# Attention and a routed feed-forward layer on one core: the ScalarE and VectorE programs of attention written out for all 64 heads, and the last stage's weights, tokens and first masks prepared inside attention

## The reference

```python
xn = layernorm(x)
q, k, v = (xn @ W.T + b for each)            # 16 heads of 16 features, q scaled by 1/4
att = softmax(q @ k.T) @ v @ Wo.T + bo       # per batch and head, over 2048 keys
route = top2-masked softmax(xn @ wg + bg), divided by its sum over the batches
seq_ids = top_k(route per expert and batch, 1024)
out = scatter-add over 16 experts of gelu(xn @ w1 + b1) @ w2 + b2     # 64 hidden units each
x + att + layernorm(xn + out) * gamma + beta
```

## Time and profile before

| | |
|---|---|
| three runs | 3382.39, 3384.15, 3384.7 us (median 3384.15) |
| the profiled execution | 3384.77 us |
| its span, first to last instruction | 3383.0 us |
| busy in the span | TensorE 97%, VectorE 86%, ScalarE 75%, GpSimd 28% |
| mean granted TensorE clock | 0.989 of full speed |
| attention, first to last score matmul | 257.5 to 2913.4 us |
| first matmul of the last stage | 2925.1 us |
| loads of weight pieces, issue to landing (median) | 256 KB 7.9 us, 512 KB 9.0 us |
| VectorE's reciprocal of the last sums, 128x512 | 3.35 us |

### The profile page before, as it was taken

The page is one execution under the profiler, slowest core; times in us unless marked ns, Lnnn a source line. Parts: engine busy times, 40 slices in busy tenths (PEclk is TensorE's granted clock), DMA queues, the critical chain, the costliest instruction groups (busy, mean ns, idle before and its releaser), DMA issues. The chain is left out here.

```text
span 3383.0 us, 75004 instructions
## 1 busy us (share of the span) xinstructions
PE 3289.2 (97%) x20848; PEld 1702.7 (50%) x20848; DVE 2901.3 (86%) x2989; ACT 2524.3 (75%) x5724; POOL 933.5 (28%) x1340
## 2 busy tenths in 40 slices
PE   7999999999999999999999999999999999799998
PEld 6444444444444444444444444444444444488887
DVE  7758899999999999999999999999999998377777
ACT  3557788888888888888888888888888888544333
POOL 2550222222222222222222222222222222244443
PEclk9999999999999999999999999999999999899999
DMA  5783333333333333333333333333333332455554
GB/s 197 200 236 47 54 55 54 55 54 55 55 59 58 57 57 59 59 55 59 55 55 54 54 54 55 54 54 55 54 55 57 58 58 42 117 158 158 166 158 118
DMA packets 140694, 271.93 MB, mean 80 GB/s; under 512 B 30192, under 2 KB 76336, under 8 KB 128112
## 3 DMA queue, kind: packets, MB, share of 16 engines
q1 hardware_dynamic: 138144, 266.71, 37.4%
q10 hardware_dynamic: 2256, 1.36, 0.2%
HBM read 173.59 MB, written 84.93 MB: 76 GB/s over the span
## 5 line engine op out<-in xcount | busy, mean ns | idle before, releaser
L921 DVE TENSOR_REDUCE half_max<-m_ps 128x1 f32<-128x1024 f32 x2006 | 2363.5, 1220 | 223.9 <-PE m_ps L848 212.0
L802 ACT ACTIVATE prob<-s_ps 128x512 f32<-128x512 f32 (+1 forms) x5120 | 2191.1, 521 | 425.6 <-PE s_ps L858 417.0
L858 PE MATMUL s_ps<-q_feat,k_feat 50*128 50x512 f32 (+1 forms) x5120 | 1542.9, 397 | 13.8 <-ACTq L792 5.9
L848 PE MATMUL m_ps<-k_feat,q_feat 48*128 48x512 f32 x4012 | 1358.8, 444 | 20.3 <-DVE half_max L921 20.2
L858 PEld LDWEIGHTS s_ps<-q_feat,k_feat 50*128 50x128 f32 x5120 | 798.8, 185 | 994.7 <-ACT prob L802 880.9
L867 PE MATMUL a_ps<-prob,v_head 128*32 128x512 f32 x8192 | 1096.2, 607 | 0.0
L848 PEld LDWEIGHTS m_ps<-k_feat,q_feat 48*128 48x128 f32 x4012 | 599.0, 186 | 221.7 <-DVE half_max L921 211.3
L657 POOL TENSOR_TENSOR shift<-row_max,shift 128x16 fp32r<-128x16 f32 x63 | 14.0, 222 | 1164.1 <-ACT shift L809 1164.1
L867 PEld LDWEIGHTS a_ps<-prob,v_head 128*32 128x32 f32 x8192 | 161.4, 108 | 256.3 <-issue 217.8
L1221 ACT ACTIVATE g_hi<-g 128x512 fp32r<-128x512 f32 x128 | 81.0, 632 | 251.0 <-DVE g L1263 210.8
L1385 POOL TENSOR_TENSOR g_lo<-g,g_hi 128x512 fp32r<-128x512 f32 x128 | 173.5, 1355 | 224.3 <-ACT g_hi L1221 224.2
(11 more groups left out here) (147 smaller groups left out, 2000.5 us busy)
## 6 DMA issues: line engine op xcount, KB each, us to landing
q_feat<-q_parts SPq DMA_DIRECT2D x384, 128.0 KB, 4.2
k_feat<-k_parts SPq DMA_DIRECT2D x384, 128.0 KB, 5.6
q_parts<-parts SPq DMA_DIRECT2D x32, 512.0 KB, 4.3
k_parts<-parts SPq DMA_DIRECT2D x32, 512.0 KB, 4.4
att_dram<-att SPq DMA_DIRECT2D x64, 256.0 KB, 6.3
mask_bc<-mask_b SPq DMA_DIRECT2D x128, 128.0 KB, 4.5
x_in<-in_x SPq DMA_DIRECT2D x16, 512.0 KB, 4.2
xn_dram<-xn SPq DMA_DIRECT2D x16, 512.0 KB, 4.8
```

Source lines behind the costliest of these rows:

```text
L802: act.activation(prob[tile(r, kt) % R][:, cols(j)], s_ps[slot(r, kt, j) % R][:, wide(j)], ACT.Exp).then_inc(exped, 1)
L848: ins = pe.matmul(m_ps[p % 2][:, k * BLK:(k + 1) * BLK], q_feat[r % 2][LOW, qt * P:(qt + 1) * P], k_feat[r % 2][LOW, key:key + BLK], start ...
L858: pe.matmul(s_ps[slot(r, kt, j) % R][:, wide(j)], k_feat[r % 2][UP, kt * P:(kt + 1) * P], q_feat[r % 2][UP, cols(j)], start=True, stop=Tru ...
L921: dve.tensor_reduce(half_max[r][:, p // 2, p % 2:p % 2 + 1], m_ps[p % 2][:, :], AX.X, ALU.max).then_inc(maxed, 1)
```

## The change

ScalarE's program of attention becomes one line of 64 written-out heads, and VectorE's writes out the maxima of heads 2 to 63; both loops go. The loops of TensorE, GpSimd and SyncE stay.

The tensors of the last stage that can be filled early are laid over `v_all`: its memory is taken, released, and taken again by `w1_hi`, `w2_lo`, `w2_hi`, `xn_hi0`, `xn_lo0`, `woT_sb`, `wo_hi`, `gamma_bc`, `w1_lo`, `mask_bc0` and `b1_col`. SyncE loads w1 (1 MB) and b1 in attention after its loop, ahead of head 61's loads, and w2 (1 MB) after the mask is there, then block 0's tokens and mask quarter 0. VectorE rounds and splits both weights at the end of its attention program. In `finish` the six pieces and TensorE's waits for them are gone. SyncE's order at its start is new: it waits for the store of the last head's sums, loads the sums, then issues mask quarter 1, `quotients(0)`, `halves(1, 1)`, `tokens(0)`, and waits for b2's parts. VectorE inverts the sums in four quarters (two after gate 1, two after gate 2) and splits them after gates 3, 4 and 5.

```diff
+SUMS_AT = 4 * S
+INV_AT = SUMS_AT + BLK
+LATE_AT = INV_AT + PARTS * BLK // 2
...
+        with nc.sbuf_tensor("v_all", [P, B, H, ST, HD], F32) as v_all:
+            pass
+        w1_hi = sb("w1_hi", [P, KC, E * F], F32R)
+        w2_lo = sb("w2_lo", [P, EP, D], F32R)
...
-            v_all = sb("v_all", [P, B, H, ST, HD], ctx=first)
...
+    raw = spare[:, LATE_AT:LATE_AT + KC * E * F], spare[:, S:2 * S]
...
             sp.dma_start(sums, sum_rows(t, 0)).then_inc(sums_in, 16)
+            sp.dma_start(raw[0].rearrange("p (c n) -> p c n", c=KC), t["w1"].rearrange("(c p) n -> p c n", p=P)).then_inc(raw_in[0], 16)
+            sp.dma_start(t["b1_col"][:, :], t["b1"]).then_inc(t["b1_in"], 16)
...
             sp.dma_start(t["mask_b"], mask16).then_inc(mask_stored, 16)
+            sp.dma_start(raw[1].rearrange("p (c n) -> p c n", c=EP), t["w2"].rearrange("(c p) n -> p c n", p=P)).then_inc(raw_in[1], 16)
+            sp.wait_ge(mask_stored, 16)
+            sp.dma_start(t["xn_hi0"][:, :].bitcast(F32).rearrange("p (n s) -> p n s", n=KC),
+                         t["tok_hi_dram"][0:KC].rearrange("n p s -> p n s")).then_inc(t["xn_in"][0], 16)
+            sp.dma_start(t["xn_lo0"][:, :].bitcast(F32), t["tok_all"][:, 0, :]).then_inc(t["xn_in"][0], 16)
...
+            for k in range(2):
...
+                sp.dma_start(first_masks[k * F:(k + 1) * F, :, :],
+                             src.unsqueeze(0).broadcast_to([F, EP // 4, BLK])).then_inc(t["masks_in"][0], 16)
             sp.wait_ge(inverted, 1)
...
-            step(0, 0, first=True)
-            step(1, 1)
-            with nc.Fori(0, ROUNDS, engines=[ENGINE.Activation], hint_back_edge=True, head_slot={ENGINE.Activation: 40}) as i:
-                for r in range(2, U + 2):
-                    step(i * U + r, r)
-            for g in range(2 + ROUNDS * U, HEADS):
-                step(g, g, following=g + 1 < HEADS)
+            for g in range(HEADS):
+                step(g, g, first=g == 0, following=g + 1 < HEADS)
             collect(HEADS - 1)
...
-            maxima(2, 2)
-            with nc.Fori(0, ROUNDS, engines=[ENGINE.DVE], hint_back_edge=True, head_slot={ENGINE.DVE: 16}) as i:
-                for k in range(U):
-                    maxima(i * U + R + k, k % R)
-            maxima(HEADS - 1, (HEADS - 1) % R)
+            for n in range(2, HEADS):
+                maxima(n, n % R)
...
+            dve.wait_ge(masked, 1)
+            for k, (hi, lo) in enumerate(((w1_hi, w1_lo), (w2_hi, w2_lo))):
+                dve.wait_ge(raw_in[k], 16)
+                dve.tensor_copy(hi, raw[k]).then_inc(raw_rounded, 1)
+                dve.wait_ge(raw_rounded, k + 1)
+                dve.tensor_tensor(lo, raw[k], hi.bitcast(F32), ALU.subtract).then_inc(weights_split, 1)
...
-            load_w1(0)
-            halves(0, 0)
-            load_w2(0)
-            masks(0, 0)
...
+            sp.wait_ge(t["att_out"], 16 * (HEADS + 1))
+            sp.dma_start(sums[:, :], sum_rows(t, 1)).then_inc(sums_in, 16)
             masks(0, 1)
             quotients(0)
+            halves(1, 1)
             tokens(0)
             sp.wait_ge(b2_split, 1)
             for k in range(PARTS):
                 sp.dma_start(b2_rows[k * E:(k + 1) * E, :], b2_parts[:, k, :]).then_inc(b2_placed, 16)
-            sp.wait_ge(t["att_out"], 16 * (HEADS + 1))
-            sp.dma_start(sums[:, :], sum_rows(t, 1)).then_inc(sums_in, 16)
-            halves(1, 1)
...
-            for dst, src in ((b2_sb[:, :], t["b2"]), (b1_col[:, :], t["b1"]), (gamma_bc[:, :], t["gamma"].partition_broadcast(P))):
+            for dst, src in ((b2_sb[:, :], t["b2"]), (gamma_bc[:, :], t["gamma"].partition_broadcast(P))):
...
-            for k in range(AHEAD_PIECES):
-                round_piece(k)
             act.activation(t["warm"][:, :], t["ident"][:, 0:1], ACT.Gelu)
-            act.wait_ge(small_in, 16 * 3)
+            act.wait_ge(t["b1_in"], 16)
...
-                    if not last and e == 4:
-                        invert_sums()
-                    if not last and e == 5:
-                        split_inverses()
+                    if not last and 1 <= e <= 2:
+                        invert_sums(2 * e - 2)
+                        invert_sums(2 * e - 1)
+                    if not last and 3 <= e < 2 + PARTS:
+                        split_inverses(e - 3)
+                    if not last and e == 2 + PARTS:
+                        last_inverses()
```

More of the change, by code:

```diff
@@ L65 @@
 HALVES = NBLK * KC
+SUMS_AT = 4 * S
+INV_AT = SUMS_AT + BLK
+LATE_AT = INV_AT + PARTS * BLK // 2
+LATE_LEFT = (B - 1) * H * ST * HD - (LATE_AT + KC * E * F + BLK + EP)
 class Chain:
@@ L621, in attend @@
     gt, eq, cum = (spare[0:B * E, k * S:(k + 1) * S] for k in range(3))
+    w1_hi, w1_lo, w2_hi, w2_lo = (t[w][:, :, :].rearrange("p c n -> p (c n)") for w in ("w1_hi", "w1_lo", "w2_hi", "w2_lo"))
+    raw = spare[:, LATE_AT:LATE_AT + KC * E * F], spare[:, S:2 * S]
+    raw_in, raw_rounded, weights_split = t["raw_in"], t["raw_rounded"], t["weights_split"]
     mask16 = spare[0:B * E, 3 * S:3 * S + S // 2].bitcast(BF16)
-    sums = spare[:, 4 * S:4 * S + BLK]
-    inv_parts = spare[:, 4 * S + BLK:4 * S + BLK + PARTS * BLK // 2].bitcast(BF16).rearrange("p (k s) -> p k s", k=PARTS)
+    sums = spare[:, SUMS_AT:INV_AT]
+    inv_parts = spare[:, INV_AT:LATE_AT].bitcast(BF16).rearrange("p (k s) -> p k s", k=PARTS)
     TREE = 8
@@ L962, in finish @@
     AHEAD = 2
[L963 to L970, removed]
+    w1_hi, w1_lo, w2_hi, w2_lo, woT_sb, wo_hi = (t[w] for w in ("w1_hi", "w1_lo", "w2_hi", "w2_lo", "woT_sb", "wo_hi"))
+    gamma_bc, b1_col = t["gamma_bc"], t["b1_col"]
+    wo_lo = sb("wo_lo", [P, KC, D], F32R)
     b2_sb, b2_left = sb("b2_sb", [E, D]), sb("b2_left", [E, D])
@@ L975, in finish @@
     spread = sb("spread", [H * PARTS, D], BF16)
-    mask_bc = [sb(f"mask_bc{q}", [P, QTR, BLK], BF16) for q in range(2)]
+    mask_bc = [t["mask_bc0"], sb("mask_bc1", [P, QTR, BLK], BF16)]
     mask_rows = sb("mask_rows", [PARTS * E, BLK], BF16)
@@ L980, in finish @@
     base = sb("base", [P, TPB, D])
-    xn_hi = [sb(f"xn_hi{u}", [P, KC * BLK], F32R) for u in range(2)]
-    xn_lo = [sb(f"xn_lo{u}", [P, KC * BLK], F32R) for u in range(2)]
+    xn_hi = [t["xn_hi0"], sb("xn_hi1", [P, KC * BLK], F32R)]
+    xn_lo = [t["xn_lo0"], sb("xn_lo1", [P, KC * BLK], F32R)]
     g = [sb(f"g{r}", [P, BLK]) for r in range(2)]
@@ L1015, in finish @@
     sums_in, inv_chain, sums_inverted, inverses_stored = sem("e_sums_in"), sem("e_inv_chain"), sem("e_sums_inverted"), sem("e_inverses_stored")
-    masks_in = [sem(f"e_masks_in{q}") for q in range(2)]
+    masks_in, xn_in = t["masks_in"], t["xn_in"]
     loaded = sem("e_loaded")
     num_in = sem("e_num_in")
-    xn_in = [sem(f"e_xn_in{u}") for u in range(2)]
     hidden = sem("e_hidden")
@@ L1230, in block_step @@
                     hidden_units(blk, e)
-                    if first and AHEAD_PIECES + e < len(pieces):
-                        round_piece(AHEAD_PIECES + e)
                     if first and e == 4:
@@ L1312, in add_quotients, with invert_sums, split_inverses, last_inverses @@
                                       ALU.add).then_inc(added, 1)
-            def split_piece(k):
-                src, hi, lo = pieces[k]
-                dve.wait_ge(piece_rounded, k + 1)
-                dve.tensor_tensor(lo, src, hi.bitcast(F32), ALU.subtract).then_inc(piece_split, 1)
-            do = Chain(dve, inv_chain)
-            def invert_sums():
-                dve.wait_ge(sums_in, 16)
-                do(dve.reciprocal(sums[:, :], sums[:, :]))
-            def split_inverses():
-                for k in range(PARTS - 1):
-                    do(dve.tensor_copy(inv_parts[:, k, :], sums[:, :]))
-                    do(dve.tensor_tensor(sums[:, :], sums[:, :], inv_parts[:, k, :], ALU.subtract))
+            do = Chain(dve, inv_chain, BLK // P)
+            def invert_sums(k):
+                dve.wait_ge(sums_in, 16)
+                part = sums[:, k * P:(k + 1) * P]
+                dve.reciprocal(part, part).then_inc(inv_chain, 1)
+            def split_inverses(k):
+                dve.wait_ge(inv_chain, BLK // P + 2 * k)
+                do(dve.tensor_copy(inv_parts[:, k, :], sums[:, :]))
+                dve.tensor_tensor(sums[:, :], sums[:, :], inv_parts[:, k, :], ALU.subtract).then_inc(inv_chain, 1)
+                do.n += 1
+            def last_inverses():
+                dve.wait_ge(inv_chain, BLK // P + 2 * PARTS - 2)
                 dve.tensor_copy(inv_parts[:, PARTS - 1, :], sums[:, :]).then_inc(sums_inverted, 1)
@@ L1333, in gates @@
                     gate(blk, e)
-                    if not last and AHEAD_PIECES + e < len(pieces):
-                        split_piece(AHEAD_PIECES + e)
-                    if not last and e == 4:
-                        invert_sums()
-                    if not last and e == 5:
-                        split_inverses()
+                    if not last and 1 <= e <= 2:
```

(3 more changed lines are left out.)

46 lines of the change are left out of this document (17 added, 29 removed).

## The result

| | before | changed |
|---|---|---|
| median of four runs | 3384.1 us | 3340.18 us (3339.88 to 3341.94) |
| profiled execution, its span | 3384.77, 3383.0 us | 3341.94, 3340.2 us |
| ratio, 95% interval | | 0.9872 (0.9855 to 0.9889) |

43.9 us less, where 34 were forecast; the range 3343 to 3365 misses it by 2.8 us. The sign and the places were right; one term was missing (a steady cost of VectorE's loop, 5.6 us), and two were too small.

The account below looks back on a forecast made before the run. The prediction took TensorE to be full, with ScalarE and VectorE close behind. Attention's 21.6 us and the last stage's start, 13.1, made 34.7 off 3384.77: 3350.1 us, range 3343 to 3365.

Parts of the forecast that it names:

- TensorE is full: Attention's steady part: relieving only ScalarE's or VectorE's sequencer can't buy much; ScalarE's register instructions going gives nothing.
- The 22.6 us over the pace: Attention, 62 heads: 2572.66 us against 2550.06 at 41.13 a head; 1.0 us left to loops that stay.
- Back edges of ScalarE: nothing: Attention: ScalarE makes up for its loop's back edges at its own slack, so removing them gains nothing.
- 21.6: Attention's sum in us: 2.95 + 10.52 + 3.58 + 4.5, from both loops' entries, ScalarE's exit and VectorE's back edges.
- ScalarE's entry and exit: Attention: writing ScalarE out returns 10.52 us at loop entry, partly VectorE's, and 3.58 at the exit, read as fetching.
- The last stage's start, 13.1: Border of attention and last stage: b2 split 11.3 us earlier, 1.8 from three transfers moved; mask quarter 2 lands 13.1 earlier.
- The early loads and splits: In attention: loading and splitting the last stage's weights early costs nothing; VectorE's four instructions take 10 to 15 us.
- as long as now: Last stage: the blocks after the second keep their present length.
- (1): Rival, a price of straight code itself: 4 in 100, and 3 more for a milder form ending within 0.2%.
- (2): Rival: only the named gaps come back; attention gives 13 us, the last stage 13: 3359 us; 17 in 100.
- (3): Rival: the last stage's start gains little, 5 us instead of 13.1: 3358 us; 12 in 100.
- 23 if all of it does: Upper bound in us of attention's gain, if all the loss over the pace comes back; the lower was 13.

Follow-up runs that it names:

- act_loop: The changed kernel with ScalarE's loop put back (10 rounds over heads 2 to 61), VectorE written out and all preparation kept: 3348.99 us.
- dve_loop: The changed kernel with VectorE's loop put back (10 rounds over the maxima of heads 3 to 62), ScalarE written out: 3356.45 us.
- prep_only: The changed kernel with both loops put back, so the preparation of the last stage alone: 3370.22 us.
- wait_moved: The changed kernel with VectorE's wait for the shift of three heads ago moved from the head's first maximum to its sixth: 3340.09 us.
- two_waits_more: The changed kernel with two constant, long satisfied waits added ahead of VectorE's first maximum of each head: 3346.07 us.

## Why the prediction was wrong

**"So nothing that only relieves ScalarE's or VectorE's sequencer in the steady part can buy much: TensorE is full."** For ScalarE the sum says it again ("Its register instructions go too: nothing, TensorE is full"), and there it held: with its loop back, 30 heads take the same time to 0.5 us. For VectorE the sum has no such term at all. This is the step that failed: VectorE's register instructions cost 5.6 us over 62 heads, and without them the result would have been 3345.8 us, inside the range. TensorE is full in the mean over three heads (busy 123.37 of 124 us), but it isn't what bounds each step. The page had the sign of it, TensorE waiting for the maxima; a look at the one step in which VectorE does something besides its two maxima would have shown 0.21 us of waiting at each head, of which 0.09 go when the register instruction does.

**The 22.6 us over the pace.** The count was right, and it all came back. I had left 1.0 of it to the loops that stay; it came back too. It is ScalarE's: 0.1 us in the second head of each of the ten rounds, present in `act_loop`, absent in `dve_loop`. "Back edges of ScalarE: nothing" was wrong by that, and "21.6" mis-sized.

**ScalarE's entry and exit.** Right in place and cause, shown by moving the loop. As terms they are less certain than I wrote them: 10.52 and 3.58 were one execution's stalls with their low-clock phases. With ScalarE's loop alone, or moved, the entry costs 5.9 and 7.9; with both loops in `prep_only` 11.3. The exit costs 1.2, 5.4 and 1.2 there.

**The last stage's start, 13.1.** It gave 16.0. The chain was the right one: b2's first issue comes 12.7 us after the border (2901.46), where I had 13.6, and 24.9 before. In this execution hide(0) ran at full clock, 1.55 us instead of the 2.56 I took; that was luck, as in ten of the twelve kernels with the preparation the clock fell for some 3.4 us within 3 us of the border, and with this order of loads gate 4 came 19.4 to 21.0 us after it, around the 21 I had named. 1.3 us more came between gate 4 and `project`, where I had "all as before": TensorE's pause there was 2.3 us instead of 4.5, and the low clock after it 3.4 us instead of 6.8. The quarter's landing took 4.08 instead of 4.94.

**Costed at nothing.** The early loads and splits: right, the last split ends at 2869.7, 15 us before the last scores; a split of 128x2048 took 2.29 us and its rounding 1.22, so the four took 7.0 us where I had 10 to 15. The half more that I allowed for another engine at work beside VectorE does occur in the kernel before: `gate` (L1263) takes 0.68 us with GpSimd idle all the while (median of 50) and 1.32 us with GpSimd busy for over half of it (median of 77). What the two engines share is not shown. Quarter 1 and the sums were never late. The later blocks, "as long as now": wrong by 1.1 us, which took back part of the rest.

**Rivals.** (1) A price of straight code itself, with 4 and 3 in 100, did not show: with every head written out, no gap of ScalarE or VectorE is over 0.43 us between 300 and 2830 us. (2) and (3), both smaller gains, did not happen. The range had its ends from the same two terms, and both came out near or above their upper ends: 16.0 against 17, and 28.5 against "23 if all of it does", since an upper end taken from the losses over the quiet pace can't hold a gain in the pace.

By terms: 34.7 forecast; + 5.6 (VectorE's pace) + 1.3 (entry, exit and rest of the rounds, 28.5 - 5.6 - 21.6) + 2.9 (border) - 1.8 (blocks, with the last interval) + 0.3 (end) = 43.0, against 42.8 measured between the profiled executions.

## What to carry to other kernels

When a loop of one engine is written out, look for its cost in three places: the stall at the first entry, the stall some instructions after the exit, and every point in the body where the engine is the last to arrive, even once in sixteen steps. There count the sequencer instructions between two of the engine's own: here one was free and the second was paid at every head. Read the quiet pace as a quantity that may change, and don't take the losses over it as the upper end. A transfer that is late behind a wait may be just as late behind other loads: move it ahead of both.

## What the runs showed of the hardware

A satisfied wait can cost time, and so can a register instruction. With none or one sequencer instruction between VectorE's row maximum and its next maximum the second starts 0.103 us after the first (`wait_moved`, the changed kernel); with two it starts 0.176 us (two semaphore instructions, `two_waits_more`) or 0.186 us after it (a register and a semaphore instruction, the kernel before), and a head takes 0.08 to 0.09 us longer.

The low clock after a pause is not fixed by the pause. After ScalarE's entry stall of 4.80 us TensorE's granted clock was 0.50 for 13.7 us in the kernel before (from 352.1 us, in the earlier trace rows); after the same stall, 4.87 us, it was 0.50 for 6.8 us in `act_loop` (columns as in the earlier trace rows; the granted clock is the number behind the last bracket):

```profile
341.40:348.20 6.80, 4.88 (x20) 2.22 (x22) 2.36 (x2) 4.09 (x9) 0.17 (x1) 0.50 0.65 143
```

At the last stage's start TensorE pauses 3.0 us in every kernel with the preparation. In the changed kernel's first execution and in `two_waits_more` no low clock followed, in the other ten one of 3.4 us did; the changed kernel's two executions:

```profile
2888.00:2892.00 4.00, 1.73 (x8) 1.45 (x9) 0.00 (x0) 1.50 (x3) 1.70 (x4) 1.00 0.35 107
```

```profile
2889.40:2892.80 3.40, 3.40 (x10) 2.61 (x9) 0.69 (x1) 1.75 (x5) 0.23 (x1) 0.50 0.98 246
```

The same goes for head 0, which starts at half clock in every profiled execution: the low clock there ended at 270.4 us in one execution of the changed kernel and at 264.5 in the other. Over the twelve experiments it lasted 13.7 to 23.9 us, and the interval from the first to the second split grows with it, from 40.2 to 43.8 us. Attention starts anywhere from 253.5 to 257.5 us. These two make a good part of the 2 to 4 us by which most executions of one kernel differ; what decides them is open.
